# A causal attention layer on one NeuronCore: preparing two kinds of later batches one tile later

## The chip, the cores and the metric

The kernel runs on one core of one Trainium2 chip. The metric is device time in microseconds (us). Three timed runs of the kernel before gave 1380.26, 1382.33 and 1384.09 us; their median is 1382.33 us.

## The reference, cut to what matters

Input is x of shape (4, 512, 128): B = 4 batches of S = 512 positions. Four layers follow each other, each adding its output to x: a state space layer, a feed-forward block with attention, a causal attention layer with a triangular solve, and the same feed-forward block again. The third is the one that the change concerns:

```python
# 16 heads of 8 columns; q, k, v from layernorm(x)
q, k = rotate_first_two_columns(q), rotate_first_two_columns(k)
logits = einsum('bhqd,bhkd->bhqk', q, k) * 8 ** -0.5
probs = softmax(logits + causal_mask, axis=-1)
L = eye(s) - tril(probs, -1)
rhs = diagonal(probs)[..., None] * v
A = solve_triangular(L, rhs, lower=True)
x = x + (A.transpose(0, 2, 1, 3).reshape(b, s, 128) @ Wd.T + bd)
```

The last layer (`ffn_phase`, the second time) needs, for each batch, layernorm of x, and q and k from it; its first two batches are prepared already while the causal layer still runs.

## The kernel before, in words

The causal layer is `delta_phase` (line 2023). A batch has TPB = 4 tiles of 128 positions, so the layer has 16 tiles, n = 0 to 15, and the tile's place in its batch is t = n % 4. The loop runs over n from -6 (LEAD = 6) to 15, on every engine in the same way, and each pass (called "tile n" here) has 14 hooks, h = 0 to 13. No scheduler moves anything: each engine executes its instructions in the order in which its loop writes them, and waits at semaphores.

In tile n the solve of tile n itself runs: TensorE (PE) forms the right side (`from_earlier`, L3058, for t > 0; `inverse`, L3086), and then seven hops (L3099), each a group of 32 small matmuls that waits for a 32x32 transpose on VectorE (DVE, L2858), at hooks 3, 5, 7, 9, 10, 11 and 12. After the last, ScalarE (ACT) copies the solution (`solved`, L2592), which ends the tile.

Around this chain, tile n also works for later tiles:

- the scores of tile n + 3 (`score`, L2958, L2961 and L2970 on PE; `exponential`, L2539 and L2544 on ACT). A batch's last tile has t = 3 and the most of them: 4 groups of its own block and 16 of 128x384 elements. It is scored in tiles 0, 4, 8 and 12;
- the row maxima of tile n + 4, or of n + 3 where a batch begins (L2933 and L2936 on PE, L2701 on DVE). In tiles 1, 5 and 9 these are the two first tiles of the next batch (12 reductions of 512 columns); in tiles 0, 4, 8 and 12 there are none. In tiles 13 to 15 the maxima of the last layer's first batch take the place (`next_for_maximum` L2943, L2707);
- the products of the score blocks with the block inverses (`multiplied`, L3004), hooks 9 to 12;
- on GpSimd (POOL), the inverses of the 16x16 blocks of tile n + 2 (L2338 to L2356, 31 steps).

Batch b is prepared ahead in three stages, at the tiles where `goes_on(n, lead)` gives b, that is at n = 4b - lead - ahead(b):

- lead 6: DVE normalizes x (L2631 statistics, L2637, L2643, POOL's power L2324, L2655 at hook 10), PE transposes it (`turn_in`, L2896, hook 12), ACT copies it (L2487 or L2489), and for b < 4 PE projects the values (L2903, hook 13), which DVE takes (L2661);
- lead 5: PE projects q and k (L2911, hooks 0 and 1), ACT adds the bias (L2496);
- lead 4: for b < 4 DVE rotates q and k (two shuffles L2668, two products L2672, two L2676, two sums L2681, hooks 0 to 3) and makes their product (L2685), from which PE takes the diagonal scores (L2917, hook 7; L2695). For every b, q and k are split into three bfloat16 parts each: six casts on ACT (L2510, hooks 3 to 8) and four subtractions on DVE (L2690, hooks 4 to 7). SyncE (SP) stores the parts to DRAM (`store_parts`, L2381, six DMAs).

Batches 4 and 5 are the last layer's first two batches. The stored parts of batch b are loaded as operands of the scores (`operands`, L2395 and L2398) in tile 4(b - 1), once tile 4b - 1's scores have been formed.

SP also carries the block inverses: it stores the scores' diagonal blocks and loads them (L2410, L2414, for POOL), stores the inverses and loads them (L2418, L2425, for PE), and moves the shifts (L2404), all in the order of its loop.

Of the kernel before, what the change touches and what calls it, by code (L numbers as in the profile page):

```python
# [2022 lines left out]
def delta_phase(core, nc):  # L2023
# [4 lines left out]
    with ExitStack() as ctx:  # L2028
# [176 lines left out]
        def values_at(b):  # L2205
            return (1 - LEAD, 2) if b == 0 else (TPB * b - LEAD - ahead(b), 13)
# [30 lines left out]
            return in_program(n) and n % TPB >= 2  # L2237

        def ahead(b):
            return (0, 0, 2, 4, 4, 4)[b]  # L2240

        def goes_on(n, lead):

            return next((b for b in range(B + 2) if TPB * b - lead - ahead(b) == n), None)
# [977 lines left out]
```

How the kernel before makes its waits and increments, by code:

```python
        @block.sync  # L158
        def _(sp):
            n = 0
            x_tiles = core.dram["in_L0_attn_a_x"].rearrange("b (n p) h -> p (b n) h", p=P)
            for dst, src in [(core.x[:, :, :], x_tiles)] + [(core.w[k], core.dram[k]) for k in core.w if not k.startswith("m_")]:
                sp.dma_start(dst, src).then_inc(loaded, 16)
                n += 16
            sp.wait_ge(loaded, n)
            blank_regions(core, sp, "f1_")
            blank_regions(core, sp, "f3_")
# [145 lines left out]
                def store_rows(b):  # L313
                    sp.wait_ge(s["xp_sb"], b + 1)
                    sp.dma_start(core.bc_scr[b], xp[b % 2][DT_RANK:ROWS, :]).then_inc(rows_out[b], 16)
# [1 line left out]
                def load_chunk(c):  # L317
                    b, k = divmod(c, CHUNKS)
                    if k == 0:
                        sp.wait_ge(rows_out[b], 16)
                    if c >= RING:
                        last = CHUNK * (c - RING) + CHUNK
                        sp.wait_ge(s["hC_dve_out"], dve_states(last))
                        sp.wait_ge(s["hC_pool_out"], pool_states(last))
                    src = core.bc_scr[b, 2 * CHUNK * k:2 * CHUNK * (k + 1), :].rearrange("r s -> (r s)")
                    sp.dma_start(ring[:, c % RING, :, :, :].rearrange("p c r s -> p (c r s)"),
                                 src.unsqueeze(0).to_broadcast([P, 2 * CHUNK * S])).then_inc(ring_in[c % RING], 16)
# [100 lines left out]
                def turned(b):  # L428
                    act.wait_ge(s["xT_ps"], b + 1)
                    if b >= 2:
```

## Time and profile before

| what | value |
|---|---|
| median of three timed runs | 1382.33 us |
| the profiled execution's own time | 1384.38 us |
| its span, first to last instruction | 1382.3 us |
| PE, DVE, ACT, POOL busy | 1162.0, 982.6, 686.8, 619.0 us |
| mean granted TensorE clock over the span | 0.901 of full |

The profiled execution took 2.05 us more than the median. Tile n of the causal layer is taken from the start of the one solution copy (L2592) to the next; the first starts at 721.9 us and the last at 1079.7 us, 358 us of the span. The other layers hold no instruction that the change touches. In the tables of stretches, PEclk 1.00 is the full granted clock (2.4 GHz) and 0.50 the half (1.2 GHz).

### The profile page before, as it was taken

What the parts mean: (1) busy time and instruction counts of PE and PEld (TensorE: products, weight loads), DVE (VectorE), ACT (ScalarE), POOL (GpSimd) and SP (SyncE); (2) the same over time, 40 slices, a digit from 0 to 9 for tenths busy, and PEclk for the clock granted to TensorE, in tenths of its full rate; (3) what the DMA queues carried; (4) which work ended last, traced back from release to release, by engine and by line L of the source; (5) the groups of instructions that cost most, each with busy time, mean ns of one, the idle gap of its engine ahead of it and who ended that gap; (6) DMA issues with size and microseconds to landing.
All of it is one profiled execution on the core that took longest, in us unless ns stands there. A gap on an engine that the chain in (4) does not pass through costs nothing. (4 is left out here: it accounts for less than half of the span.)

```text
span 1382.3 us, 33189 instructions
## 1 busy us (share of the span) xinstructions
PE 1162.0 (84%) x12998; PEld 630.4 (46%) x13034; DVE 982.6 (71%) x2128; ACT 686.8 (50%) x1425; POOL 619.0 (45%) x828
## 2 busy tenths in 40 slices
PE   6846668768999998797887888988989999999875
PEld 2212333323333334774465666666666433333375
DVE  5699999988888884545775674645735688888453
ACT  3844344414776767441362352442441377776754
POOL 2359889965234321541452353352442243432153
PEclk9968989997999999898899888979988799999988
DMA  4387934231231402227133223223132303140223
GB/s 149 123 297 298 350 154 180 79 79 35 60 93 51 120 9 87 60 75 136 25 70 68 47 46 89 31 62 74 33 81 49 72 2 93 48 123 10 87 59 90
DMA packets 132800, 127.65 MB, mean 92 GB/s; under 512 B 86295, under 2 KB 117847, under 8 KB 128122
## 3 DMA queue, kind: packets, MB, share of 16 engines
q1 hardware_dynamic: 124592, 117.65, 30.0%
q0 software_dynamic: 2496, 5.13, 1.2%
q10 hardware_dynamic: 5558, 2.76, 0.9%
q8 instruction: 103, 1.69, 0.5%
q14 instruction: 51, 0.42, 0.1%
HBM read 104.83 MB, written 37.90 MB: 103 GB/s over the span
## 5 line engine op out<-in xcount | busy, mean ns | idle before, releaser
L1480 DVE TENSOR_REDUCE f_row_min<-f_ps 128x1 f32<-128x512 f32 x480 | 308.1, 682 | 54.5 <-PE f_ps L1811 53.8
L1361 ACT ACTIVATE f_e<-f_ps 128x512 f32<-128x512 f32 x512 | 279.2, 598 | 124.6 <-PE f_ps L1830 123.8
L816 PE MATMUL m_ps<-m_shared,sb_ident 128*128 128x512 f32 x256 | 134.1, 671 | 55.2 <-DVE m_shared L664 53.1
L379 POOL TENSOR_TENSOR m_drive<-m_du,m_ring 128x1024 f32<-128x1024 f32 x64 | 149.6, 2351 | 51.0 <-DVE m_ps L656 32.2
L522 ACT ACTIVATE m_ps<-m_delta,m_A 128x511 f32<-128x511 f32 x128 | 82.9, 681 | 118.7 <-DVE m_ps L656 98.2
L1841 PE MATMUL f_ps<-f_e,f_v_op 128*32 128x512 f32 x1024 | 137.3, 608 | 2.4 <-ACT f_e L1361 1.4
L2701 DVE TENSOR_REDUCE d_row_min<-d_ps 128x1 f32<-128x384 f32 (+3 forms) x176 | 104.6, 632 | 26.4 <-PE d_ps L2936 25.3
L816 PEld LDWEIGHTS m_ps<-m_shared,sb_ident 128*128 128x128 f32 x256 | 51.5, 212 | 139.8 <-DVE m_shared L664 81.8
L656 DVE TENSOR_TENSOR_SCAN m_ps<-m_ps,m_drive 128x1024 f32<-128x1024 f32 x44 | 101.1, 2297 | 5.0
L1811 PE MATMUL f_ps<-f_second_ops 72*128 72x512 bf16 x256 | 98.0, 383 | 2.8 <-DVE f_row_min L1480 2.8
L1830 PE MATMUL f_ps<-first_ops 75*128 75x512 bf16 x256 | 99.5, 389 | 0.0
L1811 PE MATMUL f_ps<-first_ops 72*128 72x512 bf16 x224 | 92.3, 421 | 8.4 <-DVE f_row_min L1480 6.2
L1830 PE MATMUL f_ps<-f_second_ops 75*128 75x512 bf16 x256 | 92.2, 381 | 2.6 <-ACT f_e L1361 2.6
L2933 PE MATMUL d_ps<-first_ops 96*128 96x128 bf16 (+3 forms) x256 | 67.3, 328 | 14.5 <-DVE d_row_min L2701 6.7
L3099 PE MATMUL d_ps<-d_mT,d_a_hop 16*32 16x16 f32 (+3 forms) x3584 | 68.9, 210 | 12.3 <-DVE d_a_hop L2858 8.1
L2344 POOL TENSOR_TENSOR d_prod<-d_xT_blk 128x14 f32<-128x14 f32 (+6 forms) x224 | 63.0, 281 | 17.5
L2349 POOL TENSOR_TENSOR d_xT_blk<-d_xT_blk,d_prod 128x14 f32<-128x14 f32 (+6 forms) x224 | 62.1, 277 | 17.5
L1215 POOL DMA_INDIRECT f_rows_scr<-f_h2n,f_place_u x32 | 31.8, 992 | 82.7 <-DVE f_place_u L1598 75.1
L3099 PEld LDWEIGHTS d_ps<-d_mT,d_a_hop 16*32 16x32 f32 (+1 forms) x3584 | 53.3, 117 | 31.1 <-issue 16.2
L1399 ACT ACTIVATE first_ops<-f_ps,first_ops 128x128 f32<-128x128 f32 x184 | 52.6, 369 | 27.3 <-PE f_ps L1897 27.3
L2338 POOL TENSOR_TENSOR d_xT_blk<-d_e_blk,d_zi_blk 128x256 f32<-128x256 f32 x16 | 14.4, 899 | 115.5 <-DVE d_zi_blk L2773 110.0
L2544 ACT ACTIVATE d_e_off<-d_ps 128x384 f32<-128x384 f32 (+1 forms) x112 | 55.7, 552 | 17.1 <-PE d_ps L2970 16.9
(319 smaller groups left out, 2297.5 us busy)
## 6 DMA issues: line engine op xcount, KB each, us to landing
m_ring<-bc_scr SPq DMA_DIRECT2D x32, 1024.0 KB, 5.4
f_rows_scr<-blank SPq DMA_DIRECT2D x2, 8707.5 KB, 31.0
f_wall<-f_wall SPq DMA_DIRECT2D x16, 578.0 KB, 5.1
first_ops<-q_scr SPq DMA_DIRECT2D x28, 288.0 KB
first_ops<-k_scr SPq DMA_DIRECT2D x84, 96.0 KB
f_second_ops<-q_scr SPq DMA_DIRECT2D x16, 288.0 KB
f_second_ops<-k_scr SPq DMA_DIRECT2D x48, 96.0 KB
f_second_ops<-f_rows_scr SPq DMA_DIRECT2D x36, 64.5 KB, 1.8
```

Of the source, the lines that this page charges most:

```text
L379: nc.gpsimd.tensor_tensor(drive[:, step % AHEAD, :].rearrange("p (a s) -> p a s", a=HALVES), du[:, :, tokens(b)], b_row(step).unsqueeze(1) ...
L522: last = nc.scalar.activation(ps[:, at + 1:at + S], delta[:, k, b * S + 1:(b + 1) * S], ACT.Exp, scale=A[:, k, n:n + 1])
L656: nc.vector.tensor_tensor_scan(h, bank(DECAY + HALVES * (step % 2), HALVES), drive[:, step % AHEAD, :], 0.0, ALU.mult, ALU.add).then_inc(s ...
L816: last = nc.tensor.matmul(bank(Y + k), core.ident[:, :], hC[:, k * S:(k + 1) * S], start=False, stop=last_of_batch)
L1361: nc.scalar.activation(e_sb[:, n % 3, hh, :], ps[:, SCORE[(b * UNITS + u) % SCORE_BANKS], :], ACT.Exp, scale=SCALE).then_inc(s["e_out"], 1)
L1480: nc.vector.tensor_reduce(row_min[:, b % 2, u // TPB, u % TPB:u % TPB + 1], ps[:, MAXQ[unit(b, u) % MAX_BANKS], :], AX.X, ALU.max, negate= ...
L1811: nc.tensor.matmul(ps[:, MAXQ[n % MAX_BANKS], :], q_op(b, QK)[:, hd, t * P:(t + 1) * P], k_op(b, QK)[:, hd, :], start=True, stop=True).the ...
L1830: nc.tensor.matmul(ps[:, SCORE[n % SCORE_BANKS], :], k_op(b, QKS)[:, hd, t * P:(t + 1) * P], q_op(b, QKS)[:, hd, :], start=True, stop=True ...
L1841: last = nc.tensor.matmul(ps[hh * HEAD_COLS:(hh + 1) * HEAD_COLS, O_BANK, :], v_of(b, t, g * GROUP + hh), e_sb[:, n % 3, hh, :], start=(t ...
L2701: nc.vector.tensor_reduce(row_min[:, n % 2, g * heads:(g + 1) * heads], dve_bank("maximum", n, g)[:, 0:heads * cols].rearrange("p (h c) -> ...
L2933: nc.tensor.matmul(bank[:, hh * cols:(hh + 1) * cols], q_op[0:SHIFT_AT, hd, rows_of(t)], k_op[0:SHIFT_AT, hd, 0:cols], start=(hh == 0), st ...
L3099: last = nc.tensor.matmul(ps[q * SPAN:(q + 1) * SPAN, STEP[n % 2], r * SPAN + cols.start:r * SPAN + cols.stop], a_hop[own, g * SPAN:(g + 1 ...
```

## The change

One line of numbers: the batches 3, 4 and 5 are prepared 3 tiles ahead of the fixed leads in place of 4. Batch 2 stays where it was.

```diff
         def ahead(b):
-            return (0, 0, 2, 4, 4, 4)[b]
+            return (0, 0, 2, 3, 3, 3)[b]
```

| stage | before: tiles for b = 3, 4, 5 | now |
|---|---|---|
| lead 6: normalize, turn, project values (b = 3) | 2, 6, 10 | 3, 7, 11 |
| lead 5: project q and k | 3, 7, 11 | 4, 8, 12 |
| lead 4: rotate (b = 3), split, store | 4, 8, 12 | 5, 9, 13 |

PE at the end of tile 3 and the start of tile 4: L3099 is the last hop of tile 3, L3049 and L2981 are the output and the sums that open tile 4, L2958 and L2961 its first scores.

```order
 L3004 MATMUL d_ps<-d_xT,d_e_nat 32x16 x4
-L3099 MATMUL d_ps<-d_mT,d_a_hop 32x16 x16
+L2896 MATMUL d_ps<-sb_ident,d_swap 128x128 x4
+L3099 MATMUL d_ps<-d_mT,d_a_hop 32x16 x16
+L2903 MATMUL d_ps<-sb_d_wqkv,d_rest 128x128 x4
 L3049 MATMUL d_ps<-sb_d_wd,d_aT 128x128
 L2981 MATMUL d_ps<-d_e_off,sb_ones_at 32x128 x32
+L2911 MATMUL d_ps<-d_rest,sb_d_wqkv 128x512 x2
 L2958 MATMUL d_ps<-sb_mask_diag,sb_ident_b 128x512
 L2961 MATMUL d_ps<-first_ops 128x128 x4
```

The transposes and the values' projection of batch 3 came from the same place one tile earlier, and the projection of q and k from hooks 0 and 1 of tile 3.

DVE from the right side (L2849) of tile 5 on, before: L2858 are the hops' transposes, L2701 the maxima of tile 8.

```order
L2849 TENSOR_TENSOR d_g_pad<-d_ps,d_vn 128x4x4x8
L2755 TENSOR_TENSOR d_z_col<-d_z_col,d_ps 128x16
L2858 STREAM_TRANSPOSE d_a_hop<-d_ps 128x4x8
L2766 TENSOR_TENSOR d_z_spread<-d_z_col,sb_blocks 128x128
L2701 TENSOR_REDUCE d_row_min<-d_ps 128x4
L2858 STREAM_TRANSPOSE d_a_hop<-d_ps 128x4x8
L2701 TENSOR_REDUCE d_row_min<-d_ps 128x4
L2773 RECIPROCAL d_zi_blk<-d_ps 128x16
L2701 TENSOR_REDUCE d_row_min<-d_ps 128x4 x2
```

The same stretch now:

```order
L2849 TENSOR_TENSOR d_g_pad<-d_ps,d_vn 128x4x4x8
L2668 STREAM_SHUFFLE d_swap<-d_qk 128x512
L2672 TENSOR_TENSOR d_qk<-d_qk,sb_cos 128x512
L2676 TENSOR_TENSOR d_swap<-d_swap,sb_sin 128x512
L2755 TENSOR_TENSOR d_z_col<-d_z_col,d_ps 128x16
L2676 TENSOR_TENSOR d_swap<-d_swap,sb_sin 128x512
L2681 TENSOR_TENSOR d_qk<-d_qk,d_swap 128x512
L2858 STREAM_TRANSPOSE d_a_hop<-d_ps 128x4x8
L2766 TENSOR_TENSOR d_z_spread<-d_z_col,sb_blocks 128x128
L2701 TENSOR_REDUCE d_row_min<-d_ps 128x4
L2681 TENSOR_TENSOR d_qk<-d_qk,d_swap 128x512
L2858 STREAM_TRANSPOSE d_a_hop<-d_ps 128x4x8
```

Five instructions of the rotation now stand between the right side and the first hop's transpose, and a sixth before the second.

SP in tile 5: L2404 are the shifts of tiles 8 and 9, L2418 and L2425 the inverses of tile 7, L2410 the blocks of tile 8.

```order
L2404 DMA first_ops<-d_max_part 3x16x128 x2
L2381 DMA q_scr<-d_part 16x8x512
L2381 DMA k_scr<-d_part 16x8x512
L2381 DMA q_scr<-d_part 16x8x512
L2381 DMA k_scr<-d_part 16x8x512
L2381 DMA q_scr<-d_part 16x8x512
L2381 DMA k_scr<-d_part 16x8x512
L2418 DMA x_scr<-d_xz_blk 128x256
L2425 DMA d_xT<-x_scr 16x16x16 x8
L2410 DMA e_scr<-d_e_nat 16x16x16 x8
```

The six stores stand between the shifts and the inverses now; before, they came at the end of tile 4, behind the loads of batch 2's operands and ahead of the inverses of tile 6.

## Rows read from the trace of the kernel before

**Rows 1.** The page's first part: busy us, share of span, instructions, by engine.
```profile
PE 1162.0 (84%) x12998; PEld 630.4 (46%) x13034; DVE 982.6 (71%) x2128; ACT 686.8 (50%) x1425; POOL 619.0 (45%) x828
```

**Rows 2.** Busy time by stretch: tiles 2 to 5; columns as in its header.
```profile
core 0: us, PE busy (x) PEld busy (x) DVE busy (x) ACT busy (x) POOL busy (x), PEclk, DMA share, GB/s
...
752.30:781.60 29.30, 22.43 (x538) 16.82 (x538) 26.46 (x72) 11.88 (x26) 10.43 (x30) 0.83 0.21 35
781.60:809.10 27.50, 25.77 (x614) 18.62 (x616) 16.51 (x42) 11.03 (x25) 11.13 (x34) 0.93 0.21 41
809.10:834.10 25.00, 22.06 (x528) 17.70 (x529) 13.87 (x32) 13.77 (x33) 12.76 (x33) 0.71 0.41 88
834.10:859.40 25.30, 21.81 (x579) 17.09 (x584) 12.14 (x39) 5.12 (x15) 9.71 (x31) 0.88 0.34 81
```

**Rows 3.** Timeline of PE in tile 2: start, us, what; idle before, releaser in brackets.
```profile
761.07 0.34 PE L2933 MATMUL d_ps<-first_ops 96*128 96x384 bf16 x1 [1.87 <-DVE d_row_min L2701]
...
778.24 0.45 PE L3099 MATMUL d_ps<-d_mT,d_a_hop 32*32 32x32 f32 x32 [1.12 <-DVE d_a_hop L2858]
...
779.63 1.12 PE L2896 MATMUL d_ps<-sb_ident,d_swap 128*128 128x128 f32 x4
...
781.42 2.08 PE L2903 MATMUL d_ps<-sb_d_wqkv,d_rest 128*128 128x128 f32 x8
```

**Rows 4.** Timeline of DVE in tile 2, the normalization.
```profile
763.82 0.87 DVE L2631 BATCH_NORM_STATS2 d_stats<-x 128x6 f32<-128x128 f32 x4
...
776.74 1.32 DVE L2655 TENSOR_SCALAR d_swap<-x,d_mv,d_rstd 128x128 f32<-128x128 f32 x4
```

**Rows 5.** Timeline of PE at the ends of tiles 6 and 10.
```profile
877.60 0.61 PE L3099 MATMUL d_ps<-d_mT,d_a_hop 32*32 32x32 f32 x32 [1.30 <-DVE d_a_hop L2858]
...
978.75 0.66 PE L2896 MATMUL d_ps<-sb_ident,d_swap 128*128 128x128 f32 x4
```

**Rows 6.** Timeline of PE in tile 3: the projection of q.
```profile
788.09 1.13 PE L2911 MATMUL d_ps<-d_rest,sb_d_wqkv 128*128 128x512 f32 x2
```

**Rows 7.** Timeline of PE in tiles 6 and 8.
```profile
873.17 0.67 PE L3004 MATMUL d_ps<-d_xT,d_e_nat 128*32 128x112 f32 x32
...
919.68 0.72 PE L2970 MATMUL d_ps<-first_ops 128*128 128x128 bf16 x6 [0.56 <-ACT d_e_off L2544]
...
926.74 1.11 PE L3004 MATMUL d_ps<-d_xT,d_e_nat 128*32 128x112 f32 x32 [0.26 <-ACT d_e_off L2544]
```

**Rows 8.** Busy time by stretch, at full and at half clock (columns as rows 2).
```profile
815.30:823.10 7.80, 6.66 (x148) 4.81 (x146) 6.66 (x16) 7.07 (x16) 4.54 (x9) 1.00 0.25 27
823.10:840.20 17.10, 15.51 (x377) 13.45 (x381) 2.67 (x8) 5.57 (x15) 6.88 (x23) 0.50 0.74 189
922.10:939.10 17.00, 15.11 (x365) 13.02 (x369) 2.61 (x8) 5.51 (x15) 6.86 (x22) 0.50 0.64 160
1017.60:1031.30 13.70, 12.26 (x318) 10.14 (x319) 2.26 (x8) 5.17 (x14) 6.57 (x21) 0.50 0.63 164
```

**Rows 9.** Timeline of DVE in tiles 4 and 5.
```profile
811.25 0.69 DVE L2672 TENSOR_TENSOR d_qk<-d_qk,sb_cos 128x512 f32<-128x512 f32 x1
...
818.32 1.94 DVE L2690 TENSOR_TENSOR d_rest<-d_qk,d_part 128x512 f32<-128x512 f32 x2
...
843.51 0.22 DVE L2858 STREAM_TRANSPOSE d_a_hop<-d_ps 128x32 f32<-128x32 f32 x1 [1.13 <-PE d_ps L3086]
```

**Rows 10.** Timeline of SP's queue behind tiles 2 and 5, and of POOL.
```profile
782.37 0.60 SPq L2381 DMA_DIRECT2D k_scr<-d_part  x1
783.25 0.36 SPq L2418 DMA_DIRECT2D x_scr<-d_xz_blk  x1
785.13 4.81 SPq L2425 DMA_DIRECT2D d_xT<-x_scr  x8
...
859.69 4.82 SPq L2425 DMA_DIRECT2D d_xT<-x_scr  x8
...
873.17 0.86 POOL L2338 TENSOR_TENSOR d_xT_blk<-d_e_blk,d_zi_blk 128x256 f32<-128x256 f32 x1 [1.84 <-DMA d_e_blk<-e_scr]
```

## Prediction

> **What bounds the kernel now.** I read the page first: TensorE is busy for 84% of the span and VectorE for 71% [rows 1], so PE's work and what PE waits for decide. The change touches the 358 us of the causal layer alone, so I cut it into tiles by the copy that ends each, and asked for the busy time of each tile [rows 2]. The reader is to see three kinds. Tile 2 is DVE's: 26.46 us busy of 29.3. Tile 3 is PE's: 25.77 of 27.5. Tile 4, in which the last tile of a batch is scored, has both free for a while, PE 22.06 and DVE 13.87 of 25.0, and a mean granted clock of 0.71. Tile 5 looks as if DVE were free, 12.14 of 25.3; but that is an average. Its timeline shows DVE idle for long until the right side and late in the tile, and in between, from 843.5 to 853.8 us, one instruction behind the other with no idle time over 0.2 us: the twelve maxima, the splitting of the minima, and the hops' transposes. A PE hop waits there for a transpose that stands behind maxima in DVE's order. What is added in that stretch lengthens the tile; what is added elsewhere in tile 5 does not.
>
> Then I asked where the clock falls. In tile 4 it is full from 815.3 to 823.1, while ACT is busy for 7.07 of 7.80 us, and half (1.2 of 2.4 GHz) from 823.1 to 840.2; the same follows in tiles 8 and 12, at 922.1 and 1017.6 [rows 8]. Just before each of these falls PE waited again and again for ACT, which had six casts of the split between the exponentials: in tile 8 five waits, the longest 0.56 us, 2.2 us together [rows 7]. The product of 32 matmuls takes 1.11 us at the half clock and 0.67 at the full one [rows 7], so the half clock costs 40% of PE's busy time in it.
>
> The sum is made against the profiled execution, 1384.4 us; the median of three runs lies 2.05 us lower, and I carry that over.
>
> **Part by part.**
>
> *Tiles 2, 6 and 10 lose the normalization, the turn, and tile 2 the values.* In tile 2 DVE is packed, and PE waited 1.12 us for the transpose that stands behind the normalization of 1.32 us, and 1.87 us for a maximum earlier [rows 3, 4]. I count 1.1 for the first, 0.9 for the statistics (0.87), 1.1 for the turn and 2.1 for the values' projection, which PE does one after the other at the tile's end [rows 3]: 5.2 us. In tile 6 the wait was 1.30 us [rows 5], the turn costs 1.1 at its clock, as in tile 2, and I count 0.4 of the statistics, since PE is nearly full there: 2.8. In tile 10 the turn takes 0.66 at full clock [rows 5]; 1.0 with the same 0.4. Sum: -9.0. Bounds: -4 if DVE is late anyway, -12 if the half clock at the ends of tiles 2 and 6 also goes.
>
> *Tiles 3, 7 and 11 take them over and lose the projections.* The projection of q took 1.13 us and k's as much, start to start 1.1 [rows 6]: -2.2. They gain 0.4 for statistics, 1.1 for the wait behind the normalization, 0.7 for the turn at full clock: +2.2. Tile 3 also gains the values, 2.08 scaled by 0.66/1.12 to full clock: +1.2. Sum: +1.2, between 0 and +5 (all of it at half clock).
>
> *Tiles 4, 8 and 12 lose the six casts and take the projections.* +2.2 for these, and -2.2 for the waits on ACT; in tile 4 the waits are somewhat fewer, but PE also loses the diagonal scores. What is late next there is PE itself: the twelve groups of six matmuls with the hops between them (0.72 us each [rows 7]) nearly fill it. Sum: 0, within 3 each way.
>
> *Tiles 5, 9 and 13 take the split, and tile 5 the rotation.* This is the cost. One 128x512 instruction takes 0.69 us, 0.6 from start to start, a shuffle 0.75 [rows 9]. The first shuffle and product fall into DVE's idle time ahead of the right side and cost nothing. Five stand between the right side and the first hop's transpose: 3.2 us, of which 1.13 us were idle [rows 9], so +2.1. Behind it come one sum, the product and four subtractions, 3.7 us, in the packed stretch: tile 5 grows by 5.8. Queued behind them are the hops' transposes and the maxima, and PE waits for both. Tiles 9 and 13 have no rotation: four subtractions, 2.4 us each. In tile 4 two subtractions took 1.94 us, against 1.3 undisturbed, at the moment when POOL began the block inverses [rows 9]; POOL begins at the same hook in tile 5. I add 1.0 for all three tiles. ACT and PE have room for the casts and the diagonal scores (ACT was busy for 5.12 us of tile 5 [rows 2]). Sum: +11.6; from +5 (half of it under waits that are there anyway) to +13.
>
> The Trainium skill, "SBUF — State Buffer", section "Who interferes with whom", says that a VectorE instruction with two SBUF inputs and a GpSimd one that reads SBUF exclude each other, the second waiting for the whole of the first. The row of 1.94 us agrees with it. By the rule every added subtraction beside POOL's 31 steps could wait; the sum goes by the row.
>
> *SP.* The six stores now stand ahead of the inverses of tile 7 (11). Six issues of 0.65 us put off everything behind them by 3.9 us; behind the same stores in tile 2 the next store landed after 1.9 us, so the DMA rings were not what it waited for [rows 10]. The inverses of tile 7 were read from 859.7 for 4.8 us and landed some 2 us later, at 866.4; PE needed them at hook 9 of tile 6, at 873.2 [rows 7, 10]. 3.9 us later is still early. But the blocks of tile 8 also come 4 us later, and POOL already waited 1.84 us for them [rows 10]; its result is needed at hook 9 of tile 7, and I estimate the slack left there at about zero. +1.5, between 0 and +6. The stores of batch 5 in tile 13 stand where SP waits for POOL anyway. In tiles 4, 8 and 12 the inverses behind the stores come earlier, for which nobody waits.
>
> *Clock.* PE was busy for 15.51, 15.11 and 12.26 us in the three half clock stretches [rows 8]; 40% of 42.9 is 17.1 us. With the casts gone PE is full from 815 on, and I expect the fall not to come. I take 14 of the 17.1, for a tile in which it comes later. New falls: in tile 2 the clock fell right after PE's wait of 1.87 us for DVE, to a mean of 0.83 over the tile [rows 2, 3]. Tile 5 gets such a wait, tile 9 a thinner stretch. 6.8 us at half clock cost 2.7; I take that once, since PE waits for DVE in the rest. Net -11.3, between -17 and +5.
>
> The sum: -9.0 + 1.2 + 0 + 11.6 + 1.5 - 11.3 = -6.0. From 1384.4 that is 1378.4 for an execution like the profiled one, and 1376.3 for the median. Without the clock's 14 us it would be +8.0. So the change by its instructions alone is a loss: it moves DVE work from tile 4, where DVE was busy for 13.87 of 25.0 us and PE hid it, into a stretch where DVE sets the pace. Only the clock makes it a gain.
>
> The Trainium skill, "TensorE: Matmul & The Clock Gate", section "HAM oscillation — how this bites in real kernels", ties the fall to long idle gaps such as a wait for a DMA; the section "A second HAM failure mode: psum-queue depth-cycling" allows it for short idles between groups of matmuls. By the first rule waits of 0.56 us would not make the clock fall, and taking them away would bring nothing of the 14 us: 1390, the third case below, whose chance counts this reading in. The rows speak for short waits, as three tiles in three fall at the same place.
>
> **The rivals.**
>
> *The clock holds (forecast).* 1370 to 1380 around 1376.3. For it: tiles 4, 8 and 12 fall at the same place; in tiles 9 to 11 it stayed full for 78 us with the same hops. Against it: the tiles' second half is made of small matmuls.
>
> *The clock's gain goes as it comes.* It stays full in tiles 4 and 8 for longer, but falls in tiles 5, 9 and 13 behind DVE and at the ends of tiles 3, 7 and 11: half of 14 is left. 1384.4 + 5.3 + 2.7 - 7 - 2.05 = 1383, so 1379 to 1386.
>
> *DVE becomes the bound and the clock falls anyway: slower.* The place is hooks 1 to 8 of tiles 5, 9 and 13, the price 11.6 us, and it decides as soon as the clock gives back less than 8.0 us, which is what all other terms come to (slower by more than 0.3% below 4 us). +8.0 on the median is 1390. For it: the packed stretch of tile 5 is certain, and tile 2 shows what the rotation does beside maxima, 29.3 us and a fall. Against: the falls of tiles 4, 8 and 12 have a cause that the change removes.
>
> *SP's queue is late.* PE waits at hook 9 of tiles 6, 7, 10 and 11 for inverses, 4.5 us more than counted: 1381 on top of the forecast, 1387 on top of the second case. For it: the queue's slack is thin. Against: no PE wait of before names a DMA in these tiles.
>
> **How the numbers follow.** The forecast 0.45, the second case 0.20, slower by DVE 0.27, SP 0.08. A difference of 0.3%, 4.1 us, is about what a measurement of this kernel can tell from none: faster is below 1378.2, slower above 1386.5. Of the forecast 0.41 is faster and 0.04 the same; of the second 0.03 faster, 0.15 the same, 0.02 slower; the third is slower but for 0.02; SP splits 0.02, 0.03 and 0.03. That makes faster 0.46, same 0.24, slower 0.30. The range runs from 1367 (the clock's whole gain and half of DVE's cost hidden) to 1392 (the third case with SP's 1.5 doubled); the forecast's own is 1370 to 1380.
>
> **What would show each step.** Tile 2 shorter by about 5 us, tile 6 by 3. Tile 3 within 2 us of before. Tiles 4 and 8 at a mean clock near 0.9 or more, and near 20 us in place of 25. Tile 5 at 28 to 31 us with DVE busy for 20, and PE waiting for the transpose L2858 ahead of the first hop; tile 9 about 1 us longer. SP's inverses of tile 7 some 4 us later against the tile's end. I am wrong if tiles 4, 8 and 12 still show the half clock from their middle on, if tile 5 doesn't grow, or if PE waits for `d_xT`.

## The result and the profile after

The changed kernel takes **1395.05 us** (median of 12 runs, 1379.56 to 1400.18), the kernel before beside it on the same chip 1383.98 us (12 runs, 1376.19 to 1391.5). The ratio is **1.0082, 95% interval 1.0054 to 1.0110**: slower by 11 us. The prediction was 1376.3 us, a gain of 6. Executions of one kernel fall into a faster and a slower state, and every ratio in this document compares those of the faster state alone.

The profiled execution of the changed kernel took 1393.81 us. Its busy times by engine (they answer to [rows 1]):

```profile
PE 1161.2 (83%) x12998; PEld 630.1 (45%) x13034; DVE 983.4 (71%) x2128; ACT 690.1 (50%) x1425; POOL 617.7 (44%) x828
```

Every engine has the work it had. PE is busy for 0.8 us less than before, and the span is 9.5 us longer. The causal layer went from 357.8 to 367.0 us; all else from 1024.5 to 1024.8. The layer as one stretch, the kernel before first, then the changed one (columns as [rows 2]):

```profile
721.90:1079.70 357.80, 312.67 (x8092) 231.96 (x8119) 204.65 (x571) 125.70 (x298) 138.11 (x409) 0.86 0.28 58
```
```profile
722.10:1089.10 367.00, 310.29 (x8092) 229.57 (x8119) 206.41 (x571) 129.20 (x297) 136.05 (x408) 0.88 0.28 57
```

The clock is a little better, 0.88 for 0.86, and PE is busy for 2.4 us less. But PE is idle for 56.7 us where it was idle for 45.1: +11.6. In this pair of executions the loss is waiting. Tiles 2 to 5, 7 to 9 and 11 to 13 of the changed kernel ([rows 2] show tiles 2 to 5 of before):

```profile
751.80:778.60 26.80, 21.11 (x549) 15.67 (x552) 24.34 (x59) 11.33 (x25) 10.57 (x30) 0.87 0.20 31
778.60:803.60 25.00, 22.11 (x599) 16.26 (x594) 18.06 (x53) 10.48 (x24) 9.69 (x31) 0.96 0.27 57
803.60:828.60 25.00, 21.30 (x532) 15.86 (x533) 6.14 (x18) 12.61 (x28) 12.58 (x36) 0.90 0.29 55
828.60:859.10 30.50, 26.91 (x589) 20.86 (x593) 21.36 (x55) 8.70 (x22) 11.42 (x31) 0.72 0.31 64
878.20:907.40 29.20, 23.27 (x602) 17.62 (x592) 18.79 (x54) 10.37 (x24) 19.70 (x63) 0.88 0.18 30
907.40:932.40 25.00, 19.94 (x524) 14.55 (x525) 4.81 (x16) 12.63 (x28) 9.60 (x31) 0.91 0.30 64
932.40:962.00 29.60, 25.20 (x580) 19.28 (x585) 14.90 (x43) 8.53 (x21) 10.94 (x31) 0.73 0.29 59
981.20:1010.50 29.30, 22.70 (x602) 16.37 (x595) 18.56 (x55) 10.55 (x24) 18.20 (x58) 0.93 0.20 32
1010.50:1034.20 23.70, 20.89 (x524) 14.84 (x525) 5.05 (x16) 12.61 (x29) 11.05 (x35) 0.87 0.29 61
1034.20:1058.60 24.40, 19.91 (x546) 14.93 (x550) 11.60 (x29) 6.00 (x15) 10.89 (x31) 0.79 0.26 59
```

Tile 4 kept its clock (0.90 for 0.71) and is as long as before. Tile 5 has the low clock now (0.72) and is 5 us longer. Whom PE waited for in the layer, before and then after (engine, tile and line, releaser, us in total, times, longest; "issue" is a wait for nothing that the profile shows):

```profile
PE d_ps L3099 <- DVE d_a_hop L2858: 7.7, 11, 1.5
...
PE d_ps L2970 <- ACT d_e_off L2544: 4.5, 11, 0.6
...
PE d_ps L3099 <- issue: 3.4, 6, 1.4
...
PE d_ps L3004 <- issue: 1.4, 2, 0.8
```
```profile
PE d_ps L3099 <- DVE d_a_hop L2858: 10.4, 12, 1.9
...
PE d_ps L3099 <- issue: 5.3, 4, 2.3
PE d_ps L2961 <- DMA first_ops<-d_max_part: 4.4, 2, 2.3
...
PE d_ps L3004 <- DMA d_xT<-x_scr: 2.8, 1, 2.8
...
PE d_ps L3004 <- issue: 2.2, 3, 1.1
PE d_ps L2970 <- ACT d_e_off L2544: 2.2, 6, 0.4
...
PE d_ps L2981 <- issue: 2.0, 1, 2.0
...
PE d_ps L3058 <- issue: 1.2, 1, 1.2
```

ACT's casts gone: -2.3. Hops' transposes behind DVE: +2.7. SP's queue (shifts and `d_xT`): 7.2 where there was 0.4, though the operands `k_scr` cost 1.8 less. And waits without a releaser of 0.4 us and more: 10.0 in place of 5.3 us. I had no term for this last kind.

One pair of executions can't tell which of these differences the change makes. Five executions of the kernel before's layer are at hand (its own and four with other fillers ahead of the layer, experiment 7). The wait for the shifts (`first_ops<-d_max_part`) is in none of them, and it is 4.4, 2.8 and 6.4 us in three executions of the changed kernel (its own and two of experiment 7): this is the change's. The wait for `d_xT` is 0.4 to 5.2 us in the five, so the 2.8 us may be scatter. The waits without a releaser are 5.3 to 16.0 us in the five, so the 10.0 us are not shown to be more than before.

**The standstills.** Six of the changed kernel's seven of over 0.7 us in the layer (PE's timeline, tiles 6 to 14):

```profile
877.52 0.38 PE L3099 MATMUL d_ps<-d_mT,d_a_hop 16*32 16x16 f32 x25 [1.11 <-issue]
...
931.61 0.45 PE L3099 MATMUL d_ps<-d_mT,d_a_hop 16*32 16x16 f32 x17 [2.27 <-issue]
...
979.01 0.36 PE L3004 MATMUL d_ps<-d_xT,d_e_nat 128*32 128x80 f32 x17 [1.12 <-issue]
...
982.68 1.72 PE L3058 MATMUL d_ps<-d_e_off,d_a_all 128*32 128x128 f32 x51 [1.21 <-issue]
...
1037.51 0.87 PE L2981 MATMUL d_ps<-d_e_off,sb_ones_at 128*32 128x128 f32 x12 [1.99 <-issue]
...
1073.06 0.38 PE L3099 MATMUL d_ps<-d_mT,d_a_hop 32*32 32x32 f32 x22 [1.54 <-issue]
```

They begin in the middle of a group: of a hop's 32 matmuls, 25 come only after 1.11 us. The page lists a DMA queue of kind "instruction":

```profile
q8 instruction: 103, 1.69, 0.5%
```

103 packets of 16 KB; PE has 12998 + 13034 matmuls and weight loads [rows 1], so a packet holds about 256 instructions with the waits among them. I numbered PE's instructions (matmuls, weight loads and waits at semaphores) from the layer's start in five traces that have all 18547 of them (experiments 1, 2, 3, the first of 4 and the first of 7): all 39 standstills without a releaser of 0.6 us or more lie at number 209 to 212 modulo 256. And in the changed kernel each of the seven ends 1.2 to 1.7 us after a packet of that queue landed. I read this as PE standing still because its next 256 instructions aren't there yet; experiment 7 moves the boundaries and tests it.

### The profile page after: what moved, and what is told of

It reads as the page before. It is cut to its first block and busy times, and to the rows that moved or that the text cites. A ratio compares the mean times of both kernels' runs of the same rounds, so it can differ in the third digit from the quotient of the medians.

```text
span 1391.8 us, 33189 instructions
## 1 busy us (share of the span) xinstructions
PE 1161.2 (83%) x12998; PEld 630.1 (45%) x13034; DVE 983.4 (71%) x2128; ACT 690.1 (50%) x1425; POOL 617.7 (44%) x828
## 5 line engine op out<-in xcount | busy, mean ns | idle before, releaser
L2701 DVE TENSOR_REDUCE d_row_min<-d_ps 128x1 f32<-128x384 f32 (+3 forms) x176 | 104.4, 629 | 29.5 <-PE d_ps L2936 28.6
L2933 PE MATMUL d_ps<-first_ops 96*128 96x128 bf16 (+3 forms) x256 | 71.1, 344 | 13.3 <-DVE d_row_min L2701 7.3
L3099 PE MATMUL d_ps<-d_mT,d_a_hop 16*32 16x16 f32 (+3 forms) x3584 | 66.4, 206 | 16.8 <-DVE d_a_hop L2858 10.9
L3099 PEld LDWEIGHTS d_ps<-d_mT,d_a_hop 16*32 16x32 f32 (+1 forms) x3584 | 51.4, 115 | 35.3 <-issue 19.4
L2858 DVE STREAM_TRANSPOSE d_a_hop<-d_ps 128x32 f32<-128x32 f32 x112 | 23.6, 210 | 57.0 <-PE d_ps L3099 50.2
```

The source lines that it names most:

```text
L2701: nc.vector.tensor_reduce(row_min[:, n % 2, g * heads:(g + 1) * heads], dve_bank("maximum", n, g)[:, 0:heads * cols].rearrange("p (h c) -> ...
L2933: nc.tensor.matmul(bank[:, hh * cols:(hh + 1) * cols], q_op[0:SHIFT_AT, hd, rows_of(t)], k_op[0:SHIFT_AT, hd, 0:cols], start=(hh == 0), st ...
L3099: last = nc.tensor.matmul(ps[q * SPAN:(q + 1) * SPAN, STEP[n % 2], r * SPAN + cols.start:r * SPAN + cols.stop], a_hop[own, g * SPAN:(g + 1 ...
```

## The experiments

Ratios are to runs of the kernel before on the same chip, with 95% intervals. They are not the quotients of the two medians: these come out at 1.0006 in experiment 1, 0.9979 in 2 and 1.0051 in 3, where the ratios are 1.0049, 1.0011 and 1.0105, and the kernel before's own executions spread over 2% there (1365.21 to 1396.81 us beside experiments 1 and 2). So a difference of less than 0.5% between two experiments decides nothing by itself.

A tile's length comes from one execution, and single executions of one kernel scatter: in the five executions of the kernel before the layer took 355.1 to 365.7 us, and tile 14 17.3 to 22.7 us, with where the clock happened to fall. The profiled executions of experiments 1, 2 and 3 (1374.46, 1370.79 and 1376.20 us) were 6, 6 and 13 us shorter than the medians of their kernels. So ratios decide on totals, and tiles only on places.

**1. The split later, and nothing else.** In the kernel before:

```diff
-return next((b for b in ... if TPB * b - lead - ahead(b) == n), None)
+return next((b for b in ... if TPB * b - lead - ahead(b) + (lead == 4 and b >= 3) == n), None)
```

> The kernel before with only the last stage (rotation, split, stores) of batches 3, 4 and 5 one tile later, in tiles 5, 9 and 13; normalization, turn and projections stay in tiles 2, 3, 6, 7, 10, 11. Tiles 4, 8, 12 lose the casts and take nothing in. My prediction's term was 2.2 us of waits and 5 to 6 us of clock for each of them: they would come to 17 or 18 us in place of 25. Rival B (banks): with the clock full, PE waits for ACT to empty one of the two banks instead, since scores, exponentials and products alternate, and the tiles only come down to 22 or 23 us. Tile 5 about 30, tile 9 about 29 us in both. Whole: by the prediction's term 1372 or less where before has 1384; by rival B with SP's late queue 1386 to 1392.

Measured: 1.0049 (1.0016 to 1.0082). Tiles 3 to 5:

```profile
778.30:805.60 27.30, 25.67 (x616) 18.48 (x616) 16.48 (x42) 10.98 (x25) 11.90 (x37) 0.94 0.22 44
805.60:824.40 18.80, 16.33 (x521) 12.39 (x521) 5.23 (x16) 11.19 (x27) 10.54 (x33) 1.00 0.28 52
824.40:854.90 30.50, 26.24 (x593) 19.80 (x593) 21.25 (x55) 8.66 (x21) 11.76 (x32) 0.78 0.35 78
```

Without the casts the clock stays full through tile 4, which takes 18.8 us (25.0 before); tiles 8 (with 3.4 us at half clock) and 12 take 20.1 and 18.9. That part of the forecast was nearly right (17 or 18 us). Tile 5 takes the gain back: 30.5 for 25.4. Tiles 4, 5, 8, 9, 12 and 13 together take 142.4 us, for 143.9 before.

**2. The casts cut down, nothing moved.** The kernel before with ACT's casts of the batches 3, 4 and 5 at 32 of 512 columns; the rest of their split is left out.

```diff
-nc.scalar.copy(part[:, i, j, :], (rest if j else qk)[:, i, :])
+nc.scalar.copy(part[:, i, j, few], (rest if j else qk)[:, i, few])   # few: 32 columns for b >= 3
```

> The kernel before, the six casts of batches 3, 4 and 5 cut to 32 of 512 columns (the split is not computed for the rest): ScalarE's load of tiles 4, 8 and 12 goes, nothing is added anywhere. This is the term of the prediction alone. By the prediction: tiles 4, 8 and 12 shrink by 2 us of waits and by 4 to 6 us of clock each, to 18 or 19 us, the whole by 17 or more. By rival B (PE then waits for the banks): 2 to 3 us each, to 22 or 23 us, the whole by 6 to 9, with the clock full from 815 on all the same. If the clock still falls at 823, the casts were not its cause.

Measured: 1.0011 (0.9963 to 1.0060). Here the casts are gone, the clock no longer falls in the second half of tiles 4, 8 and 12, no work is added anywhere, and nothing is gained that can be told from zero: the interval leaves room for 5 us, where the forecast was 17 or more. Tiles 4 and 5:

```profile
803.40:823.40 20.00, 16.89 (x529) 13.25 (x530) 13.45 (x32) 11.68 (x33) 11.77 (x34) 1.00 0.32 58
823.40:853.00 29.60, 22.25 (x585) 16.54 (x585) 12.89 (x39) 5.16 (x15) 11.16 (x33) 0.88 0.50 104
```

Together 49.6 us, for 50.3 before; with tiles 8, 9, 12 and 13 it is 144.1 us, for 143.9. (This execution's layer is 350.1 us, 7.7 shorter than in the kernel before's own, but none of that lies in these six tiles.) Inside tile 5 (PE's timeline, then the stretches ahead of and in that standstill):

```profile
836.25 0.29 PE L3100 MATMUL d_ps<-d_mT,d_a_hop 16*32 16x16 f32 x6 [5.24 <-issue]
```
```profile
825.90:831.00 5.10, 4.39 (x129) 3.30 (x126) 1.05 (x5) 0.53 (x2) 0.00 (x0) 1.00 0.89 167
831.00:836.20 5.20, 0.01 (x1) 0.00 (x0) 0.40 (x1) 0.00 (x0) 0.00 (x0) 0.82 0.84 165
```

PE passed a packet boundary at 825.9. The next packet mostly starts within 1.5 us of that; this one started at 833.2, landed at 834.5, and PE went on at 836.25. In between the DMA engines were 89 and 84% busy. SP had issued the loads of the scores' operands from tile 4 on, up to 827.4 us, so I put this down to them: when tile 4 is short, tile 5 runs into them.

**3. The projections later too** (the same edit with `lead in (4, 5)`).

> Before, with the last two stages of the batches 3, 4 and 5 one tile later (the projections of q and k in tiles 4, 8 and 12, rotation and split in tiles 5, 9 and 13), and the normalization, the turn and the values where they were. It stands between the run with the last stage alone (layer 348.5 us, ratio 1.005) and the changed kernel (367.0 us, 1.008). Theory: what made tiles 4, 8 and 12 of the changed kernel 25 us and not 19 is the work between the tile's start and the inverse's use, projections above all: they come to 22 us or more here. Rival: it is the values and the turn at the end of tile 3 and the clock falling there: tiles 4, 8 and 12 stay at 19 to 20.5 us here (2.2 us of projections minus nothing), and the layer at 350 to 354 us.

Measured: 1.0105 (1.0055 to 1.0155). Tiles 4, 8 and 12 take 21.7, 24.0 and 21.5 us, each at full clock, against 18.8, 20.1 and 18.9 in experiment 1: +2.9, +3.9 and +2.6. I had priced the two projections at 2.2 us at half clock, so about 1.3 at full. In tile 8, 3.5 us of standstills are in the sum (0 in experiment 1). For the rest of the way to the changed kernel's 25.0, 25.0 and 23.7 there remain the turn and the values just ahead of the tile and the half clock at its start, which no run takes apart. The changed kernel's first 5.2 us of tile 4, and the rest of the tile:

```profile
803.60:808.80 5.20, 5.20 (x74) 4.76 (x74) 1.70 (x4) 0.00 (x0) 2.99 (x5) 0.53 0.11 29
808.80:828.60 19.80, 16.10 (x470) 11.10 (x459) 4.44 (x14) 12.61 (x28) 9.59 (x31) 1.00 0.34 62
```

**4. The stores one tile later.** The changed kernel, the six stores of the batches 3 and 4 behind the next tile's shifts:

```diff
-if goes_on(n, 4) is not None and n != 0:
+if goes_on(n, 4) is not None and n != 0 and goes_on(n, 4) not in (3, 4):
     store_parts(goes_on(n, 4))
+if goes_on(n - 1, 4) in (3, 4):
+    store_parts(goes_on(n - 1, 4))
```

> The changed kernel, but the stores of batches 3 and 4 are issued one tile later (tiles 6 and 10, behind the shifts), so that nothing of SP stands behind them in tiles 5 and 9. Theory S (SP's queue): in the changed kernel's trace PE waits 2.1 us for the shifts and 2.8 us for the block inverses in tile 7, and 2.3 us for the shifts in tile 11; these waits go, tiles 7 and 11 shrink by 4 to 5 us and by 3 to 5, and the whole runs 7 to 10 us faster than the changed kernel, so within 3 us of the kernel before or a little above. Rival D (VectorE and the clock alone made the loss): the waits go too, but the clock and the other waits fill the place, the whole stays 9 us or more above the kernel before. Rival: the stores now delay tile 8's or 12's inverses, and the gain is half.

Measured: 1.0059 (1.0020 to 1.0099), layer 358.2 us. The three waits that name SP's transfers in the changed kernel,

```profile
885.25 0.39 PE L2961 MATMUL d_ps<-first_ops 128*128 128x128 bf16 x4 [2.12 <-DMA first_ops<-d_max_part]
...
899.43 0.67 PE L3004 MATMUL d_ps<-d_xT,d_e_nat 128*32 128x112 f32 x32 [2.83 <-DMA d_xT<-x_scr]
...
990.02 0.63 PE L2961 MATMUL d_ps<-first_ops 128*128 128x128 bf16 x4 [2.27 <-DMA first_ops<-d_max_part]
```

are gone; tile 7 went from 29.1 to 26.7 and tile 11 from 29.3 to 26.5 us. I had forecast 7 to 10 us less than the changed kernel; the ratios show 3, their intervals overlap, and so the gain stands on the named waits alone. The same with the split alone moved:

> Before, with the last stage alone (rotation, split, stores) of the batches 3, 4 and 5 one tile later, and the six stores of batches 3 and 4 one tile later still, behind the shifts. If the queue of SP is what is left of the loss (theory), tile 7 gets no longer than in the run without the late stores (24.5 us) and the ratio falls from 1.005 to about 1.002. If the loss is VectorE's in tiles 5 and 9 (rival), these two stay at 30 us each and the ratio stays at 1.005: nothing waited for SP there.

Measured: 1.0019 (0.9979 to 1.0058). Tile 7 stays at 24.5, tiles 5 and 9 at 30.5 and 28.7. The ratio came out as the theory had it, but it can't be told from experiment 1's.

**5. VectorE's work in tiles 5, 9 and 13.** The changed kernel with shuffles, products, sums and subtractions of the last stage cut to 32 of 512 columns (`[:, i, few(b)]`) for the batches 3, 4 and 5; the rest of their rotation and split is left out.

> The changed kernel with VectorE's instructions of the last stage (rotation, product, subtractions) cut to 32 of 512 columns for the batches 3, 4 and 5; the rest of their rotation and split is left out. If VectorE's added work is what lengthens tiles 5, 9 and 13 (prediction: 5.8, 3.4 and 2.4 us), they fall from 30.4, 29.7 and 24.4 to about 24, 27 and 22 us, and the ratio to before is 0.996 or less. If the clock's fall in these tiles has another cause (rival), the half clock of 17.1, 16.3 and 10.2 us in them stays and they stay within 2 us.

Measured: 1.0012 (0.9973 to 1.0052), against 1.0082: 10 us, less than forecast (0.996 or less). Tile 9 fell from 29.7 to 25.1, tile 13 from 24.4 to 21.1. The half clock in tiles 5, 9 and 13 fell from 17.1, 16.3 and 10.2 us to 6.8, 3.4 and 3.4: most of it had come with VectorE's work, against the rival. Tile 5 did not get shorter: 29.9 us with DVE busy for 14 and not 21, because PE now stood still there for 3.2 and 1.2 us at packet boundaries.

**6. The loads of the operands cut down.** One of four heads in each group loaded for the batches 2 and 3, in tiles 4 and 8; the other heads keep an older batch's operands, so their scores are not those of the reference.

```diff
-heads = slice(g * GROUP, (g + 1) * GROUP)
+heads = slice(g * GROUP, g * GROUP + (1 if 2 <= b < B else GROUP))
```

> Before, with the loads of the scores' operands of the batches 2 and 3 (tiles 4 and 8) cut to one of four heads in each group; the other heads keep the operands of an older batch. Theory (the transfers set a floor under tiles 4 and 5 together): before, where tile 4 is long, they cost little: layer shorter by 0 to 4 us, ratio 0.996 to 1.0. Rival (TensorE's own work alone sets these tiles): nothing, 0.999 to 1.001.

> The changed kernel with the same cut of the loads. Theory: 3 to 6 us less than the changed kernel, in tiles 5 and 9 (no standstill, inverses come early), ratio to before 1.003 to 1.006. Rival: VectorE alone sets tiles 5 and 9 here: they stay at 30 us, ratio 1.008.

> The run with the last stage and its stores later, with the same cut of the loads. Theory: what tile 4 gained (25 to 19 us) was given back in tile 5 because the loads, which start in tile 4, take their time whatever TensorE does, and hold up the maxima's operands, TensorE's instruction packets and the inverses: tile 5 falls from 30 to 27 us or less, tile 9 from 29 to 27, ratio 0.992 to 0.998. Rival (VectorE's rotation and split alone): tile 5 stays at 30, ratio 1.002.

Measured: before 0.9971 (0.9936 to 1.0007), changed 0.9998 (0.9956 to 1.0039), split and stores later 0.9923 (0.9888 to 0.9958). By these ratios the loads cost the kernel before 4 us (not told from none), the changed one 12 (1.0082 to 0.9998; 3 to 6 forecast) and the second one of experiment 4 some 13 (1.0019 to 0.9923). But the three were run side by side, and compared with each other they say less: the changed kernel's median is 1383.07 us, the kernel before's 1375.03, the other's 1372.29. With the loads cut in both, the change still costs 8 us, and moving the split alone gains 3 us, too little to be told from nothing. So the loads are not shown to be what turns a gain into this loss. By tiles I was half wrong: tile 5 stays at 29.6 us with DVE's work in it (29.0 in the changed kernel), only tile 9 came to 26.5 and 26.7. Tile 5 has two floors of nearly the same height, DVE and the transfers: 29.6 us in experiment 2 with the loads and without the added work, 29.6 here with the work and fewer loads, and 22.8 in the kernel before with fewer loads and no added work.

**7. Packet boundaries elsewhere.** A first try put 64 small matmuls into the first layer.

> The changed kernel with 64 more small matmuls (16 columns) on TensorE in the first layer, where it waits for others; nothing in the causal layer is changed, but TensorE's instruction stream is 128 instructions further on in it. In the changed kernel's trace TensorE stands still seven times for 0.8 to 2.3 us (10.0 us in all; before: twice, 2.2 us) with no wait for any engine, and each of these ends 1.2 to 1.8 us after a packet of 16 KB of the instruction queue landed. Theory: the instructions arrive late there; with the stream shifted by half a packet the standstills lie at other instructions and their sum is another, with the same 1.2 to 1.8 us behind a packet. Rival: they belong to these instructions (records missing, a hidden wait): they come again at the same places in the same length.

Measured: 1.0279 (1.0213 to 1.0345); it cost 23 us ahead of the layer, where PE did not wait as I had thought. Each matmul on fp32 is two in the trace, so these were 256 instructions, a whole packet, and the boundaries were where they had been: all seven standstills at number 209 to 212 modulo 256, most of them at the very matmuls of the changed kernel. That tells nothing between the two readings. Then I used fillers that are there anyway, 40 matmuls while PE waits for the layer to begin:

```diff
-for _ in range(KEPT_BUSY):
-    nc.tensor.matmul(ps[:, O_BANK, :], w["ident_b"], w["mask_diag4"], start=True, stop=True)
+for _ in range(KEPT_BUSY + 64):
+    nc.tensor.matmul(ps[:, O_BANK, 0:192], w["ident_b"], w["mask_diag4"][:, 0:192], start=True, stop=True)
```

They take 8.5 to 8.9 us in every form.

> The changed kernel with its 40 filling matmuls of 512 columns ahead of the causal layer made into 104 of 192 columns: the same TensorE time, 128 instructions more (64 matmuls, 64 weight loads). Within the causal layer the standstills of TensorE without a releaser come at every 256th instruction of its own stream (position 209 of 256 in every complete trace), behind the 16 KB packet of the instruction queue. Theory: they move to position 81, so to other instructions, and are still there at full clock, 5 to 12 us in all, because 256 instructions are executed in less time than their packet takes to come; the ratio stays at 1.003 to 1.011. Rival, luck of the place: with the boundaries elsewhere most of them vanish and the kernel is as fast as before (ratio under 1.003).

> The kernel before with the same 128 more instructions. Theory: its standstills move to position 81 and come to 3 to 9 us (5.3 before), ratio 0.998 to 1.004. Rival, luck of the place: the kernel before had a lucky place, and loses 4 us or more with this one (ratio 1.003 or more).

> The run with the last stage and the stores later (1.0019), with the same 128 more instructions. Theory: standstills 5 to 10 us (6.3 there), ratio 1.000 to 1.005; under 0.998 only if the place of the boundaries decides.

Measured: changed 1.0075 (1.0029 to 1.0121), before 0.9960 (0.9923 to 0.9998), split and stores later 0.9983 (0.9945 to 1.0021; 1.000 or more forecast). In the changed kernel each standstill lies 128 instructions off the old places (by the numbers, with the same records missing in both traces: 47 to 68 where it was 176 to 194), and they come to 13.1 us (10.0), in an execution of 1401.11 us. The largest stands in tile 5, where the changed kernel had none:

```profile
837.09 1.50 PE L3086 MATMUL d_ps<-d_xT,d_g_pad 128*32 128x128 f32 x23 [3.20 <-issue]
```

So the standstills go with the boundaries, and the change's loss is not luck of the place: beside the kernel before with the same 128 instructions (0.9960) it is larger, not smaller. But the kernel before gained, against both of my readings, so I ran it again, with 256 instructions as a control, and with 64.

> The kernel before with 128 more filling instructions once more, 0.996 (0.992 to 1.0) the first time. If the place of the packet boundaries is worth something in itself, 0.994 to 0.998 again; if that was scatter, 0.999 to 1.002.

> A control for the kernel before with 128 more instructions (0.996 and 0.995): 256 more, 168 fillers of 112 columns, so that TensorE's packet boundaries fall where they fell before. If the place of the boundaries made the gain, it is gone: 0.999 to 1.002. If the filler's form made it (a shorter or steadier wait ahead of the causal layer), 0.994 to 0.998 again.

> The kernel before with 64 more instructions (72 fillers of 272 columns), the boundaries at position 145. By the place theory it lies anywhere from 0.992 to 1.004, and its standstills lie at other instructions than in either neighbour; by the filler's form it lies between 1.000 and 0.995 as the number of fillers does.

Measured: 128 again 0.9948 (0.9917 to 0.9979), 256 1.0002 (0.9971 to 1.0033), 64 0.9951 (0.9919 to 0.9983). The control gives nothing, so the number of fillers is not the cause, and the place of the boundaries is worth up to 0.5%. The quotients of the plain medians say the same (0.9951 and 0.9964 with 128, 0.9951 with 64, 1.0003 with 256); the repeat with 128 is the weakest, since without the kernel before's executions of over 1388 us its quotient is 0.9996. Where the gain comes from I can't show: the standstills in the layer are not fewer (6.6 and 11.5 us in the two runs with 128, 11.7 with 64, 5.3 before), and the boundaries move in the last layer too. With 256 the boundaries are where they were, and the standstills came to 16.0 us in one execution: their sum says little about a kernel. These two, with 64 and with 128, are the only kernels here with the reference's result whose interval lies below the kernel before; the split moved with its stores late and 128 instructions doesn't beat them.

One thing in these runs bears on the forecast. The casts are all in place, yet the half clock of tiles 4 and 8 is 6.8 us in the repeat with 128, where it was 29.2 us: the clock still falls in the middle of both tiles, but comes back after 3.4 us. Tiles 4, 5, 8 and 9 together still take 101.7 us, for 101.0. Here too full clock in tiles 4 and 8 shortened nothing.

**8. Batch by batch** (`ahead` 3 for batch 3 alone, and for 4 and 5 alone).

> Only batch 3 prepared one tile later, batches 4 and 5 as before. Tiles 2 to 7 should look like those of the changed kernel (26.8, 25.0, 25.0, 30.4, then 7 at about 29), tiles 8 to 15 like before. If the tiles add up, the whole is 0 to 2 us above before: -2.5 -2.5 +0.1 +5.1 for tiles 2 to 5, tile 6 no gain, tile 7 +3. If the clock carries over from tile to tile, the tiles from 8 on differ from before by over 1 us each.

> The change for the batches 4 and 5 alone (tiles 6, 10, 7, 11, 8, 12, 9 and 13), batch 3 where it was. With the run for batch 3 alone at 1.0024 and the whole change at 1.008, a sum of parts gives 1.005 to 1.006; tiles 1 to 5 as before, tiles 6 to 13 as in the changed kernel, the SP wait of tile 11 (2.3 us) there, that of tile 7 (5 us) not.

Measured: 1.0024 (0.9980 to 1.0067) and 1.0024 (0.9986 to 1.0063). The two parts sum to 1.005; with their intervals that can't be told from the whole's 1.008. Neither is a gain. With batch 3 alone tile 5 takes 31.8 us, and tile 7 28.1 (PE waits 3.08 us for `d_xT`); from tile 8 on tiles differ from before by up to 2 us, no more than they do between executions. With batches 4 and 5 alone the wait for the shifts comes in tile 11 (1.90 us) and not in tile 7, as forecast.

## Why the prediction was wrong

Its steps, by the tiles of the profiled executions:

- **Tiles 2, 6 and 10, -9.0 us:** -2.5, -2.6 and -2.2, together -7.3. The sum is right in part by luck: I had -5.2 for tile 2, twice what it gained, and -1.0 for tile 10, half of it.
- **Tiles 3, 7 and 11, +1.2:** -2.5, +2.1 and +5.2, together +4.8. Tile 3, for which I had +1.2, gained instead. In tile 7 the named waits for SP's transfers (4.95 us) are more than the growth; in tile 11 they are 2.27 us of the 5.2, and 2.4 us of growth are left with late stores (experiment 4), whose cause stays open.
- **Tiles 5, 9 and 13, +11.6:** +5.0, +4.3 and +5.2, together +14.5. The mechanism was right: between 836 and 853 us of tile 5 DVE is busy for 16.45 of 17.0 us, and PE waited 1.86 us for the first hop's transpose. Experiment 5 puts this work, with the half clock that came with it, at 10 us in all.

```profile
836.00:853.00 17.00, 15.04 (x211) 10.60 (x203) 16.45 (x38) 3.99 (x8) 9.23 (x26) 0.60 0.20 34
...
839.15 0.62 PE L3099 MATMUL d_ps<-d_mT,d_a_hop 16*32 16x16 f32 x32 [1.86 <-DVE d_a_hop L2858]
```

- **SP, +1.5 with a bound of +6:** 7.2 us of named waits. I had followed the queue to the inverses of tile 7 and the blocks of tile 8; in tile 7 PE waited for the shifts of tile 10, a tile further back in the same queue, and for inverses behind them, in tile 11 for the shifts of tile 14 (experiment 4). The bound was too low, but the part that is surely the change's, the 4.4 us for the shifts, lies within it.
- **The clock, -11.3 net. This is the step that failed.** Its cause was right, and so were the falls: in tiles 4, 8 and 12 the half clock fell from 39.5 to 16.1 us. What it brings was not. I priced 14 us, most of it in tiles 4, 8 and 12 (some 15 of the 47.8 us of the three half clock stretches lie behind their ends, in tiles 5, 9 and 13); tiles 4, 8 and 12 are shorter by 0.2, and all of PE's busy time in the layer fell by 2.4. For the six tiles with the clock I had 0 + 11.6 - 11.3, so +0.3; they grew by 14.3 us, from 143.9 to 158.2 (other executions: before 144.3 to 156.0, changed 160.1 and 162.2). Experiment 2 takes this term alone, and it brings 5 us at most. Three things stand in its place. The projections, the turn and the values cost 5 to 6 us in front of each of these tiles' hops, where I had 2.2 (experiment 3). The half clock went over to tiles 5, 9 and 13, from 15.6 to 43.6 us, where I had allowed 6.8 more. Most of that came with DVE's work (experiment 5). And where PE is fast, it runs into what doesn't get faster with it: the operand loads and its own instructions in tile 5 of experiment 2, SP's queue in tiles 7 and 11 (experiment 4). How much each of the three takes stays open.

Tiles 1, 14 and 15, in which nothing changed, took 2.4 us less together; that is within what they do between executions.

The third rival, "slower by DVE while the clock falls anyway", gave 1390 and a chance of 0.27; it was the closest, and the range's end of 1392 missed by 3 us. It was right in place and near in price, but not in how the clock came into it: the clock did not fall in the middle of tile 4.

What I should have seen: rows 2 show the DMA share rise to 0.41 in tile 4 and [rows 8] 0.74 at 189 GB/s through the half clock stretch itself. I read that column for the clock alone. The loads take that time anyway, and tile 4 hid them behind slow matmuls: so I read experiment 2, though experiment 6 doesn't settle it.

The Trainium skill, "Runtime: NRT & Kernel Launch", section "Instruction fetch mechanics", says that instructions come in blocks of 16 KiB or 256 by a DMA queue of the engine's own, and calls a boundary "mostly hidden". The block and the queue agree with these traces; hidden they were not, with standstills of 5.3 to 16.0 us in five executions of the kernel before and 10.0 in the changed kernel's.

## What to carry to other kernels

Clock time that you win in a stretch is worth only what the next thing late there allows: before pricing it, read the DMA share of the stretch, and ask which transfers start in it and who needs them next. The test that settles it costs one kernel: take the suspected cause away and add nothing, as in experiment 2, before arguing over where its parts should go. Compare waits of one execution with those of other executions of the same kernel before you call them the change's. And look at a standstill that begins in the middle of a group of matmuls as instructions that come late: a kernel of many small matmuls uses up 256 of them in 3 to 4 us.

## What the hardware showed beyond that

- PE's instruction packets come late when data fill the DMA engines: in experiment 2 they mostly start within 1.5 us of a boundary, but one started 7.3 us after it, with the engines 84 to 89% busy, and PE stood still for 5.24 us.
- Where such boundaries fall in the stream is worth up to 0.5% of this kernel (0.9948 and 0.9960 with 128 instructions more, 0.9951 with 64, 1.0002 with 256).
- One subtraction of 128x512 on DVE beside POOL's first steps took 1.31 us in the changed kernel, where an undisturbed one takes 0.7; [rows 9] had shown it once.
